# A hybrid convolution and attention block: a new order of work on four engines, and the low parts of the first four turned blocks on VectorE

## The reference

```
xn   = group_norm(x)                              # 8 groups
q, k, v = qkv_w @ xn + qkv_b
x    = x + proj_w @ (v @ softmax(q.T @ k / 16).T) + proj_b
t    = tokens(x)                                  # 1024 tokens of 256
n    = layer_norm(t);  u = n / |n|
t    = t + softmax((u @ u.T) ** 2) @ n
y    = layer_norm(t) @ (sign(w - mean(w)) * mean(|w|)) + b
x    = t + round(clip(y, -1, 1) * 7) / 7          # back to channels
```

## Time and profile before

| | |
|---|---|
| time, three runs | 1971.41, 1973.5, 1975.4 us; median 1973.5 us |
| the profiled execution | 1978.41 us, of which the trace spans 1976.3 us |
| mean granted clock of TensorE | 0.962 |
| busy share of the span | PE 92%, PEld 83%, DVE 64%, ACT 47%, POOL 45% |

### The profile page before, as it was taken

The page is one execution under the profiler, slowest core; times in us unless marked ns, Lnnn a source line. Parts: engine busy times, 40 slices in busy tenths (PEclk is TensorE's granted clock), DMA queues, the critical chain, the costliest instruction groups (busy, mean ns, idle before and its releaser), DMA issues.

```text
span 1976.3 us, 34635 instructions
## 1 busy us (share of the span) xinstructions
PE 1811.1 (92%) x11810; PEld 1638.6 (83%) x11810; DVE 1267.9 (64%) x2532; ACT 936.5 (47%) x1476; POOL 880.2 (45%) x1398
## 2 busy tenths in 40 slices
PE   7999898999989999898998989989999899998987
PEld 6888888888879788797887978878888788888877
DVE  5657656576665756667576575765757667575565
ACT  3544545355453544545446354453544535355462
POOL 1633627246262552715436264362643617346271
PEclk9999999999999989999999999989999899998999
DMA  3304133050330503205042150421504124051230
GB/s 125 118 22 140 53 95 118 21 159 32 111 101 29 171 13 117 96 37 176 0 138 74 53 159 0 138 74 53 159 21 138 53 74 138 21 155 36 75 118 22
DMA packets 108575, 169.67 MB, mean 86 GB/s; under 512 B 12928, under 2 KB 79872, under 8 KB 108544
## 3 DMA queue, kind: packets, MB, share of 16 engines
q1 hardware_dynamic: 108544, 169.27, 27.2%
HBM read 85.33 MB, written 83.89 MB: 86 GB/s over the span
## 4 chain that ended last, share of the span: by engine, by line
PE 46%; POOL 23%; issue 14%; DVE 5%; ACT 5%; DMA 3%; SPq 2%; POOLq 1%; ACTq 0%; DVEq 0%
PE wide L368 16%; POOL prob L1237 5%; PE narrow L368 4%; PE wide L470 3%; PE wide L472 3%; PE wide L471 3%; PE narrow L470 3%; PE narrow L472 3%; PE narrow L471 3%; DMA e_back<-e_scratch 3%; POOL val L1276 3%; POOL ln_r L1250 2%; POOL sq_root L1264 2%; PE turn L525 2%; POOL prob L1282 2%
## 5 line engine op out<-in xcount | busy, mean ns | idle before, releaser
L368 PE MATMUL wide<-xn_hi,prob 128*128 128x512 f32 x1024 | 305.2, 399 | 0.3 <-ACT expo L727 0.3
L727 ACT ACTIVATE expo<-wide,neg_max 128x1024 f32<-128x1024 f32 x128 | 142.3, 1112 | 221.8 <-DVE neg_max L983 221.8
L1237 POOL TENSOR_TENSOR prob<-e_back,prob 128x1024 fp32r<-128x1024 f32 x64 | 153.5, 2399 | 162.4 <-ACT prob L734 161.3
L368 PEld LDWEIGHTS wide<-xn_hi,prob 128*128 128x128 f32 x1024 | 185.5, 188 | 39.1 <-ACT expo L727 0.7
L761 ACT ACTIVATE ln<-tok,ln_shift,ln_r 128x256 f32<-128x256 f32 x128 | 68.4, 592 | 297.9 <-POOL ln_shift L1252 297.9
L990 DVE STREAM_TRANSPOSE x_norm<-expo 128x1024 f32<-128x1024 f32 x128 | 158.7, 1240 | 79.0 <-ACT expo L727 77.0
L470 PE MATMUL narrow<-prob 128*128 128x256 f32 x640 | 185.8, 290 | 3.1 <-POOL prob L1237 3.1
L471 PE MATMUL narrow<-prob 128*128 128x256 f32 x640 | 182.0, 284 | 0.0
L472 PE MATMUL narrow<-prob 128*128 128x256 f32 x640 | 181.9, 284 | 0.0
L1282 POOL TENSOR_TENSOR prob<-expo,prob 128x128 fp32r<-128x128 f32 (+6 forms) x112 | 159.5, 1424 | 46.6 <-DVE prob L1023 46.6
L983 DVE TENSOR_REDUCE neg_max<-wide 128x1 f32<-128x1024 f32 x128 | 154.4, 1206 | 33.6 <-PE wide L368 33.6
(11 more groups left out here) (183 smaller groups left out, 5614.6 us busy)
## 6 DMA issues: line engine op xcount, KB each, us to landing
e_scratch<-x_norm SPq DMA_DIRECT2D x128, 512.0 KB, 3.0
e_back<-e_scratch SPq DMA_DIRECT2D x512, 128.0 KB, 3.2
x_raw<-in_x SPq DMA_DIRECT2D x32, 512.0 KB, 3.7
out<-y_sb SPq DMA_DIRECT2D x32, 512.0 KB, 3.9
tok<-in_L_conv_qkv_w SPq DMA_DIRECT2D x1, 768.0 KB, 7.0
ln<-in_L_conv_proj_w SPq DMA_DIRECT2D x1, 256.0 KB, 7.0
ln<-in_L_ffn_weight SPq DMA_DIRECT2D x1, 256.0 KB, 3.0
out_bias<-in_L_conv_proj_b SPq DMA_DIRECT2D x1, 128.0 KB, 3.7
```

What stands on the lines that cost most here:

```text
L368: mm = pe.matmul(o, lhsT, r, start=first and i == 0, stop=last and i == len(parts) - 1)
L727: act.activation(expo[:, n % DEEP], wide[n % 2][:, :], ACT.Exp, bias=neg_max[:, n:n + 1], accum_out=row_sum1[:, n:n + 1]).then_inc(e1_made, 1)
L1237: pool.tensor_sub(eT_lo[:, n % 2].rearrange("p (n i t) -> p n i t", n=NT, i=SQ), e_back[:, n % 2].rearrange("p i (n t) -> p n i t", n=NT), ...
```

## The change

Four lists change and one function goes.

- POOL: `e1T_lo` is gone there, and `gn_coefficients` stands behind `value_lo(4)` instead of behind `value_lo(0)`; the small work of the later groups stands ahead of `value_lo(2)`, `value_lo(3)` and `e2_lo(2)`.
- DVE: does `e1T_lo(0)` to `e1T_lo(3)` too, so all eight. `gn_deviation` and `gn_variance` come later; `row_max(7)` and `e1_turn(7)` come before `residual1(3)` and `cosT_lo(0)`; `cosT_lo(3)` and `cosT_lo(4)` come ahead of `e2_hi(4)` and `e2_hi(5)`.
- PE: `group_vars` stands behind `product1(3)`, `product1(4)` and both short parts of `scores2`; `product1(7)` comes before `scores2(3)`; `turn_cos(3)` and `turn_cos(4)` come before `turn_e2(3)` and `turn_e2(4)`.
- ACT: `ln2T_hi(f, 1)` before `exp1(2)`; `e1T_hi(6)` and `layer_norm1(1)` before `exp2(0)`; the later `layer_norm1`, `unit_rows` and `cosT_hi` before `exp2(3)` to `exp2(5)`.

```diff
                 turn_cos(b, 0)
+                product1(b, 3)
+                product1(b, 4)
+                scores2(b, 0)
+                scores2(b, 1)
                 if more:
                     group_vars(b + 1)
-                product1(b, 3)
-                scores2(b, 0)
-                scores2(b, 1)
-                product1(b, 4)
                 product1(b, 5)
                 turn_cos(b, 1)
                 product1(b, 6)
...
                 scores2(b, 2)
+                product1(b, 7)
+                turn_cos(b, 2)
                 scores2(b, 3)
-                turn_cos(b, 2)
-                product1(b, 7)
                 turn_e2(b, 2)
                 scores2(b, 4)
+                turn_cos(b, 3)
                 turn_e2(b, 3)
-                turn_cos(b, 3)
                 scores2(b, 5)
+                turn_cos(b, 4)
                 turn_e2(b, 4)
                 scores2(b, 6)
                 turn_e2(b, 5)
-                turn_cos(b, 4)
...
+                if f is not None:
+                    ln2T_hi(f, 1)
                 exp1(b, 2)
-                if f is not None:
-                    ln2T_hi(f, 1)
...
+                cosT_hi(b, 0)
                 exp1(b, 7)
-                cosT_hi(b, 0)
                 e1T_hi(b, 5)
+                e1T_hi(b, 6)
+                layer_norm1(b, 1)
                 exp2(b, 0)
                 exp2(b, 1)
-                layer_norm1(b, 1)
-                e1T_hi(b, 6)
...
                 row_max(b, 3)
+                e1T_lo(b, 0)
                 e1_turn(b, 3)
...
                 e1_turn(b, 4)
+                e1T_lo(b, 1)
                 residual1(b, 0)
                 if more:
                     gn_sums(b + 1, 0)
                 row_max(b, 5)
+                e1T_lo(b, 2)
                 if f is not None:
                     output(f, 1)
                 e1_turn(b, 5)
...
                 row_max(b, 6)
+                e1T_lo(b, 3)
                 e1_turn(b, 6)
                 residual1(b, 2)
+                row_max(b, 7)
+                e1T_lo(b, 4)
+                e1_turn(b, 7)
+                cosT_lo(b, 0)
+                residual1(b, 3)
+                e1T_lo(b, 5)
                 if more:
                     gn_deviation(b + 1)
-                e1T_lo(b, 4)
-                row_max(b, 7)
-                cosT_lo(b, 0)
-                e1_turn(b, 7)
+                residual1(b, 4)
+                e1T_lo(b, 6)
                 if more:
                     gn_variance(b + 1)
-                residual1(b, 3)
-                e1T_lo(b, 5)
                 e2_hi(b, 0)
                 e2_hi(b, 1)
-                residual1(b, 4)
-                e1T_lo(b, 6)
...
+                cosT_lo(b, 3)
+                e2T_parts(b, 3)
+                e2_hi(b, 4)
+                cosT_lo(b, 4)
+                e2T_parts(b, 4)
                 e2_hi(b, 5)
-                e2T_parts(b, 4)
-                cosT_lo(b, 4)
+                e2T_parts(b, 5)
                 e2_hi(b, 6)
-                e2T_parts(b, 5)
...
-            def e1T_lo(b, n):
-                pool.wait_ge(eT_hi_made, NT * b + n + 1)
...
-                e1T_lo(b, 0)
-                e1T_lo(b, 1)
...
+                if more:
+                    gn_coefficients(b + 1)
                 e2_lo(b, 4)
```

39 lines of the change are left out of this document (15 added, 24 removed).

## The result

| | before | changed |
|---|---|---|
| median, us | 1972.45 (1967.02 to 1975.4) | 1847.22 (1845.87 to 1849.51) |
| ratio, 95% interval | | 0.9369 [0.9346, 0.9392] |
| profiled execution, us | 1978.41 | 1847.24 |
| granted clock | 0.962 | 0.996 |

The change takes 125 us. The forecast was 1875 with a range from 1848, so the time lies 28 us under the forecast and 0.8 us under the range. What happened is rival A, "no low stretch comes", and the time is 3 us under A's 1850.

A forecast was written before the change was run, and what follows sets the result against it. PE bounds the kernel wherever it doesn't stall. An image of 119.93 less 6.35 gives 113.6, plus 1.5 for a low stretch 115.1, 6.2 under the mean 121.34; 16 images save 99 us, giving 1875, range 1848 to 1912.

The forecast's parts named there:

- rival A: No stretch at low clock comes: 113.6 us an image, 124 us less, 1850; chance 0.15.
- the ledger of stalls in the front: PE followed through image 8, stalls removed and added: lead over the kernel before 3.1 us at product1(5).
- The wait of 0.4 forecast for `product1(3)`: At product1(3): residual1(2) comes 0.6 later than before, so PE waits 0.4 us.
- The 0.15 for a restart: At ffn(1): 0.15 us for restarting goes along with the stall of 1.05.
- POOL and DVE in each other's way: e1T_lo(5) and e1T_lo(6) on DVE meet POOL's small steps for group 1: 0.6 us taken.
- Rival C: DVE's subtractions meet POOL's reads all eight times, 6.6 us on DVE's chain: slower than before, 1980; chance 0.05.
- `scores2(5)` waits for `cosT_lo(3)`, 0.6 ... and `scores2(6)` for `cosT_lo(4)`, 1.0: Late in the image: two new PE stalls of 0.6 and 1.0 us, each with bounds 0 and 2.5.
- I expect about one low stretch in an image, 1.5 us: About one stretch at half the clock per image, raising 113.6 us to 115.1.
- the count of pairs that would be left: New stalls left: 1.4 alone, 0.6 and 1.6 close together, 0.6 and 1.0 close together.
- The 2.8 for image 8: Low-clock cost subtracted from image 8, with 1.4 us taken per 3.40 us stretch, leaving 108.9 of PE's own work.
- rival B: Chain through e1T_hi(6) is later, waiting for fetch(6), with a second low stretch: 118 us an image, 1920; chance 0.18.

The follow-up runs named there:

- the kernel with the new tail alone: Kernel before with only the new order from scores2(2) on, on TensorE, ScalarE, VectorE and GpSimd: 1877.2 us, ratio 0.952.
- the doses on ScalarE: Changed kernel plus an unused ScalarE copy ahead of unit_rows(1): 1852.9 us with 1024 columns, 1874.7 us with 2048.
- in the tail's: Changed kernel with e2_hi(5) ahead of cosT_lo(4) and two unused VectorE reductions ahead of e2T_parts(4): 1896.1 us, ratio 0.9606.
- the kernel with the low parts on GpSimd: Changed kernel with e1T_lo(0) to e1T_lo(3) back on GpSimd: 1862.5 us, ratio 0.9418.

## Why the prediction was right and where it was wrong

**Right: the ledger of stalls in the front.** Beside the measured times, brought to the time of before by the 67.50 us: `e1_turn(4)` at 1024.80 (forecast 1024.8), `product1(2)` at 1035.13 (1035.2), `product1(5)` at 1050.11 (1050.2), `turn_cos(1)` at 1054.39 (1054.8). The stall at `product1(2)` was to be new and 1.4: it is 1.16 in image 8 and 1.39 in others. VectorE's rows show its cause: from `e1_turn(4)` to the write of the tokens its timeline has no idle time (its first and its last row):

```profile
957.30 1.25 DVE L990 STREAM_TRANSPOSE x_norm<-expo 128x1024 f32<-128x1024 f32 x1 [1.21 <-ACT expo L727]
...
967.02 0.48 DVE L1006 SCALAR_TENSOR_TENSOR tok<-narrow,inv_sum,x_tok 128x256 f32<-128x256 f32 x1
```

The wait of 0.4 forecast for `product1(3)` didn't show. `group_vars` waits 0.48 for 0.6 forecast, `turn_cos(1)` 1.17 for 1.6. The 0.15 for a restart was an estimate. At `ffn(1)` the second matmul starts 2.02 us behind the start of the last group ahead of the wait in the kernel before (1015.56 to 1017.58) and 0.70 in the changed one, which doesn't wait (948.06 to 948.76): 1.32 less, which is the idle time of 1.05 and 0.27.

**Right in kind, on the other engine: POOL and DVE in each other's way.** The forecast put 0.6 on VectorE's subtractions. All of them took 1.21 us in the mean, 128 times:

```profile
L995 DVE TENSOR_TENSOR prob<-e_back,prob 128x1024 fp32r<-128x1024 f32 x128 | 154.7, 1209 | 7.9 <-ACT prob L734 7.9
```

It is POOL that pays. Two of its small steps in image 8, and the two of VectorE's subtractions that they met:

```profile
970.81 1.09 POOL L1265 TENSOR_TENSOR len_e<-len_x,norm_eps 128x2 f32<-128x2 f32 x1
...
980.61 1.09 POOL L1244 TENSOR_TENSOR ln_v<-ln_mv,ln_eps 128x2 f32<-128x2 f32 x1 [6.78 <-DVE ln_mv L1011]
...
984.84 0.19 POOL L1265 TENSOR_TENSOR len_e<-len_x,norm_eps 128x2 f32<-128x2 f32 x1
```

```profile
970.63 1.22 DVE L995 TENSOR_TENSOR prob<-e_back,prob 128x1024 fp32r<-128x1024 f32 x1
...
980.45 1.20 DVE L995 TENSOR_TENSOR prob<-e_back,prob 128x1024 fp32r<-128x1024 f32 x1
```

A step of 0.19 us becomes 1.09, and ends 0.05 us behind VectorE's instruction (971.90 against 971.85, 981.70 against 981.65). Four such small steps per middle image, about 1 us instead of 0.19, came to 3.1 us of POOL's time. (Its busy time over fifteen images fell by 825.93 - 708.65 = 117.3 us where the sixty subtractions were 60 x 2.41 = 144.6; 1.7 us per image of shorter steps elsewhere hide part of the 3.1.) The first of the two meets `e1T_lo(3)`, so POOL was not idle at all four of the moved ones, as the prediction had it. That this cost PE 0.6 at `turn_cos(1)` isn't shown: two steps of group 1 ended 1.7 us later by it, the last of the group at 985.81, but ACT, which needs it at 985.84 for `unit_rows(1)`, was busy until 985.82 with what followed the landing of `fetch(6)`. Rival C did not come.

**Wrong in kind and size: the tail.** "`scores2(5)` waits for `cosT_lo(3)`, 0.6 ... and `scores2(6)` for `cosT_lo(4)`, 1.0". Neither wait came, and neither could under that name: by the kernel `scores2(5)` waits for `cosT_lo(2)`, `scores2(6)` for `cosT_lo(3)` and `scores2(7)` for `cosT_lo(4)`. Where VectorE is just in time is `turn_e2(5)`, as the kernel with `e2_hi(5)` ahead of the parts shows. What came is 0.78 at `turn_e2(4)` for ACT's `exp2(4)`. The lead at the start of `product2(0)` is 7.55 us (1084.25 less 1009.20 + 67.50) instead of 6.35. Inside `product2(0)` 0.7 of it is lost, 0.22 of that in the wait for POOL, a loss that the prediction didn't have; the image is 6.85 shorter.

**Wrong, the step that failed: "I expect about one low stretch in an image, 1.5 us".** This term is 24 us of the 28 by which the time was missed (1.5 x 16). The changed kernel has no such stretch in any of its fourteen middle images. Without the term the sum is 113.6 an image and 1850, which the prediction gave as rival A with a chance of 0.15; the middle images took 113.24. That A's sum comes so close owes something to errors that cancel: the tail's waits were put 0.8 us too high, and the 0.7 in `product2(0)` was left out.

The term was drawn from three cases in one trace, "0.90 with 1.45 did in image 8, and 2.47 always", and from the count of pairs that would be left. The pairs left were 0.48 with 1.17, 4.5 us apart, and 0.78 with 0.22, 9.7 us apart, and the longest single stall 1.4. The runs show that stalls of this size rarely bring a stretch (see the table) and that a single one of 2.25 mostly does. They don't give a rule by which none of 14 would have been worked out: the kernel with the new tail alone has 8 of 14 at a longest stall of 1.44. So the step is named, and that no stretch came is measured, but why the pairs left brought none where that kernel's did stays open.

Its size per stretch (1.4 to 1.5) was about right: between images with and without, 1.4 and 1.5 us in the doses on ScalarE and 1.6 in the tail's. In four other kernels the images with a stretch were longer by 0.5 to 0.9 only. The 2.8 for image 8 are two such stretches, at 1048.50 and at 1079.30, granted 0.50 and 0.51; the reason given for 1.4 each and not 1.7 doesn't hold, since PE is busy for 3.40 and 3.39 of the 3.40 us. In the second of the two stretches the matmuls of `scores2` over 512 columns take 0.63 us each and start 0.43 us apart, behind it 0.39 and 0.23; from the first start to the ninth it is 3.45 us (1079.31 to 1082.76) where eight distances of 0.23 are 1.84, so 1.6 more, the restart behind the wait included.

Two smaller things. POOL's busy share was to fall by 8 points and fell by 4, from 45% to 41%, since the span is shorter and since four of its small steps per image take about 1 us instead of 0.19. And the form of rival B, ACT and PE waiting long for `fetch(6)` with low stretches behind, is what the kernel with the low parts on GpSimd showed, at 1.1 us more per middle image than the changed kernel; its `fetch(6)` goes only 0.2 us later in the image.

What stays open: why one image of the kernel before has 3.4 us of it in its tail and the next 6.8, and what in the middle of the image brings it. In six images it stands right behind the pair at `group_vars` and `scores2(0)`, in the eight others only 10 us later, behind two more stalls.
